# Logarithm of the input factor in the exponents; one run of rotation products, sums by halves, sines ahead of the gate

## What is computed

```
proj = xn @ in_proj_w.T          # z, x, B, C, dt, theta, lam
dt = softplus(dt_raw + dt_bias);  A = -exp(A_log);  lam = sigmoid(...)
tc = cumsum(theta, axis=1)
rope(v) = [v1*cos(tc) - v2*sin(tc), v1*sin(tc) + v2*cos(tc)]
Bm, Cm = rope(rms(B)+B_bias), rope(rms(C)+C_bias)       # per head
alpha = exp(dt*A);  gamma = lam*dt;  beta = (1-lam)*dt*alpha
h_t = alpha*h + gamma*(x_t B_t) + beta*(x_{t-1} B_{t-1});   y_t = h_t C_t
y = rms((y + x*D) * silu(z), norm_w) @ out_proj_w.T
out = u + y * silu(fp8_linear(xn) + ffn_bias)
```

## Time and profile before

| | |
|---|---|
| median of three executions | 1283.85 us |
| the profiled execution | 1283.93 us, span 1282.2 us |
| busy: TensorE / VectorE / ScalarE / GpSimd | 88% / 93% / 58% / 57% |
| TensorE weight loads busy | 64% |
| DMA engines | 46.4% |
| granted TensorE clock, mean | 0.967; 1.0 throughout the units |

### The profile page before, as it was taken

One profiled execution on the slowest core, in us unless ns is written; L12 is line 12 of the kernel. 1 busy time (PEld: TensorE's weight loads), 2 busy tenths in 40 slices (PEclk: granted clock), 3 DMA queues, 4 the chain that ended last, 5 costly groups with the idle time before them and its releaser, 6 DMA issues. The chain is left out here.

```text
span 1282.2 us, 30215 instructions
## 1 busy us (share of the span) xinstructions
PE 1124.5 (88%) x11410; PEld 819.9 (64%) x11410; DVE 1195.0 (93%) x1925; ACT 737.9 (58%) x1133; POOL 736.5 (57%) x588
## 2 busy tenths in 40 slices
PE   3876499998999999999999899989999899999996
PEld 3752366766666666666666666666667666666665
DVE  7998599998999899998999899999999899989994
ACT  4776155555655565556655655556555656556553
POOL 4000166666666666565766576657666576666664
PEclk9876699999999999999999999999999999999998
DMA  8534464345544355445544454346444455434441
GB/s 187 185 99 123 111 139 102 97 93 123 126 117 97 74 146 113 100 104 108 112 107 103 114 130 102 88 96 150 108 109 91 107 122 117 100 88 90 106 98 26
DMA packets 88468, 141.26 MB, mean 110 GB/s; under 512 B 16099, under 2 KB 35268, under 8 KB 88004
## 3 DMA queue, kind: packets, MB, share of 16 engines
q1 hardware_dynamic: 88323, 139.33, 46.4%
HBM read 57.89 MB, written 12.58 MB: 55 GB/s over the span
## 5 line engine op out<-in xcount | busy, mean ns | idle before, releaser
L1412 POOL TENSOR_TENSOR rot<-part 128x512 f32<-128x512 f32 x256 | 375.5, 1468 | 507.7 <-DVE part L1220 507.1
L1220 DVE SCALAR_TENSOR_TENSOR part<-bcs,k_prmT,k_trig 128x512 f32<-128x512 f32 x512 | 502.0, 1028 | 22.1 <-DMA bcs<-bc_t 12.4
L1353 ACT ACTIVATE E<-d 128x512 f32<-128x512 f32 x256 | 151.8, 593 | 192.5 <-PE d L1051 192.5
L1062 PE MATMUL s<-rot 64*128 64x128 f32 x2048 | 150.4, 286 | 26.6 <-POOL rot L1412 26.3
L1388 ACT ACTIVATE sz<-r 128x512 f32<-128x512 f32 x128 | 76.5, 597 | 165.5 <-PE r L1137 165.4
L1062 PEld LDWEIGHTS s<-rot 64*128 64x128 f32 x2048 | 127.6, 189 | 64.6 <-issue 64.4
L1238 DVE TENSOR_TENSOR M<-s,E 128x512 f32<-128x512 f32 x256 | 163.7, 679 | 2.4 <-PE s L1062 1.8
L1421 POOL TENSOR_TENSOR ce<-rot,eb 128x512 f32<-128x512 f32 x128 | 160.1, 1271 | 0.0
L1465 POOL TENSOR_TENSOR sqa<-sqa,sq 128x512 f32<-128x512 f32 x112 | 142.5, 1272 | 16.2 <-ACT sq L1358 7.8
L1036 PE MATMUL r<-k_w_zx,xns 128*128 128x256 f32 x512 | 131.8, 383 | 12.5 <-DMA xns<-xn_t 12.5
L1149 PE MATMUL y<-M,xk 128*64 128x128 f32 x2048 | 140.1, 279 | 0.0
(11 more groups left out here) (243 smaller groups left out, 1671.1 us busy)
## 6 DMA issues: line engine op xcount, KB each, us to landing
k_trig<-k_tri SPq DMA_DIRECT2D x512, 128.0 KB, 2.4
eb<-ecum_rows SPq DMA_DIRECT2D x128, 256.0 KB, 4.7
bcs<-bc_t SPq DMA_DIRECT2D x16, 256.0 KB, 3.9
bcs<-bc_t SPq DMA_DIRECT2D x32, 128.0 KB, 3.9
a_big<-in_L_attn_u SPq DMA_DIRECT2D x4, 512.0 KB, 6.3
xn_t<-a_xnT SPq DMA_DIRECT2D x1, 2048.0 KB, 10.7
tc_t<-a_tcT SPq DMA_DIRECT2D x1, 2048.0 KB, 15.9
bc_t<-a_tmp SPq DMA_DIRECT2D x1, 2048.0 KB, 8.5
```

Of the source, the lines that this page charges most:

```text
L1062: last = nc.tensor.matmul(Sp[j][:, k], rot[rows, q % 2, p, 0, k], rot[rows, q % 2, p, 1, k], start=True, stop=True)
L1220: nc.vector.scalar_tensor_tensor(out=part[:, 2 * p + f, :], in0=bcs[:, (t + q // NQ) % 2, 2 * w + f, :], scalar=col, in1=trig[:, p, 1 - f, ...
L1353: nc.scalar.activation(E[:, h % 2, :], Dp[:], ACT.Exp).then_inc(e_ready, 1)
L1412: nc.gpsimd.tensor_tensor(rot[:, q % 2, p, w, :], part[:, 2 * p, :], part[:, 2 * p + 1, :], ALU.add).then_inc(rot_ready, 1)
```

## The change

- The factor `kk` no longer multiplies x. Its logarithm, cut in three bf16 parts, is stored to scratch (`logs_d`), loaded per slice into twelve more rows of `pick` (`OWN_L`), and so enters the exponents, which have 123 rows in place of 111. The decay to the chunk's end, `dec`, is multiplied by `kk` in `prepare`.
- `xk` is now a plain copy of x, made by ScalarE (`x_copy`, two a unit). VectorE makes only `xc`, two passes in place of four, and waits for the copy (`x_copied`).
- VectorE's list of a unit: angle, state, M 2 and 3, `x_scaled` twice, all eight products in a run, then as before.
- GpSimd's sums wait for a half of the run: sums 0 and 1 for the first four products, 2 and 3 for all eight. `ce` goes in front of the sums.
- ScalarE: copies behind the decays, then the sines, then the two Silus.
- TensorE: x 0 and x 1 one behind the other, project as a whole after them. The last project of a slice and the sum of squares move into unit 0 of the next slice; the latter goes into bank y0.
- Norm: `norm_start` behind M 3, `norm_seeded` within the run, `norm_refined` behind the squares of unit 0, `normalised` in unit 1 in front of the copies.

```diff
-D_ROWS = OWN_S + 3 * CS
+OWN_L = OWN_S + 3 * CS
+D_ROWS = OWN_L + 3 * CS
...
# prepare, GpSimd
+            for i in range(2):
+                pool.wait_ge(log_cut, i + 1)
+                nc.gpsimd.tensor_tensor(s[2]..., s[2]..., cum3[:, :, H * i:H * i + H], ALU.subtract).then_inc(log_left, 1)
+            pool.wait_ge(dec_done, 1)
+            nc.gpsimd.tensor_tensor(K["dec"][:], K["dec"][:], kk[:], ALU.mult).then_inc(log_left, 1)
# prepare, ScalarE
             for g in (0, 2):
+                if g == 2:
+                    act.wait_ge(kk_done, 2)
+                    nc.scalar.activation(s[2], kk[:], ACT.Ln).then_inc(log_left, 1)
...
+            log_part(0)
             for t in range(NS):
                 if t + 2 < NS:
                     gate_input(t + 2)
+                if t in (1, 3):
+                    log_part((t + 1) // 2)
...
+                if t in (3, 4):
+                    act.wait_ge(cum_stored, 64)
+                    for g in (2 * t - 6, 2 * t - 5):
+                        act.wait_ge(logT_t, g + 1)
+                        nc.scalar.copy(cumT[:, 1024 * g:1024 * g + 1024], ...).then_inc(logT_out, 1)
# units, TensorE
-                    if q == 0:
-                        pe.wait_ge(ssq_taken, at(1, t, 0))
...
                     exponents(t, q, 3)
+                    if q == 0 and t > 0:
+                        square_sums(t - 1)
...
                         x_by_token(t, q + 1, 0)
-                    if q > 0:
-                        project(t, q - 1, (0, 1))
                     pe.wait_ge(hch, at(T8, t, 8 * q + 8))
                     if live(t, q + 1):
                         x_by_token(t, q + 1, 1)
-                    if q > 0:
-                        project(t, q - 1, (2, 3))
+                    if t + q > 0:
+                        project(t, q - 1, range(CS))
# units, VectorE
-                dve.wait_ge(x_ready, at(T2, t, 2 * q + i + 1))
+                dve.wait_ge(x_copied, at(T2, t, 2 * q + i + 1))
...
-                    if live(t, q + 1):
-                        rotation(t, q + 1, 0, 0, 0)
-                    if q == 0 and t > 0:
-                        norm_start(t - 1)
                     if live(t, q + 2):
                         angles(t, q + 2)
                     for c in range(CS):
                         state(t, q, c)
-                    if live(t, q + 1):
-                        rotation(t, q + 1, 0, 0, 1)
-                        x_scaled(t, q + 1, tn, 0)
-                        x_scaled(t, q + 1, tn, 1)
                     scores(t, q, 2)
                     scores(t, q, 3)
                     if q == 0 and t > 0:
-                        norm_seeded(t - 1)
+                        norm_start(t - 1)
                     if live(t, q + 1):
-                        for p, w in ((1, 0), (0, 1), (1, 1)):
+                        x_scaled(t, q + 1, tn, 0)
+                        x_scaled(t, q + 1, tn, 1)
+                        for p, w in ((0, 0), (1, 0), (0, 1), (1, 1)):
                             rotation(t, q + 1, p, w, 0)
                             rotation(t, q + 1, p, w, 1)
+                            if q == 0 and t > 0 and (p, w) == (1, 0):
+                                norm_seeded(t - 1)
# units, ScalarE
+            def x_copy(t, q, i):
+                act.wait_ge(x_ready, at(T2, t, 2 * q + i + 1))
+                act.wait_ge(y_ready, at(T2, t, 2 * q - 2))
+                nc.scalar.copy(xk[:, q % 2, 2 * i:2 * i + 2, :]..., R[i][:]).then_inc(x_copied, 1)
...
                     decays(t, q, 3)
+                    if q == 1 and t > 0:
+                        normalised(t - 1)
+                    if live(t, q + 1):
+                        x_copy(t, q + 1, 0)
+                        x_copy(t, q + 1, 1)
                     if q == 0 and t > 0:
                         root(t - 1)
+                    if live(t, q + 2):
+                        sines(t, q + 2)
                     for p in range(2):
...
-                    if live(t, q + 2):
-                        sines(t, q + 2)
...
-                    if q == 0 and t > 0:
-                        normalised(t - 1)
# units, GpSimd
-                pool.wait_ge(part_ready, at(T8, t, 8 * q + 2 * k + 2))
+                pool.wait_ge(part_ready, at(T8, t, 8 * q + 4 * w + 4))
...
+                    c_decayed(t, q)
                     if live(t, q + 1):
-                        sums(t, q + 1, 0)
-                    c_decayed(t, q)
-                    if q == 0 and t > 0:
-                        norm_refined(t - 1)
-                    if live(t, q + 1):
-                        for k in range(1, 4):
+                        for k in range(4):
                             sums(t, q + 1, k)
                     if q == 0:
                         ...
+                        if t > 0:
+                            norm_refined(t - 1)
```

More of the change, by code:

```diff
@@ L217, in _ @@
             fill(cum[MASK_ROWS:OWN_T], own[MASK_ROWS:OWN_T, :], 8)
-            fill(cum[OWN_S:D_ROWS], own[OWN_S:D_ROWS, :], 8)
+            fill(cum[OWN_S:OWN_L], own[OWN_S:OWN_L, :], 8)
+            fill(cum[OWN_L:D_ROWS], own_log[OWN_L:D_ROWS, :], 8)
             by_super = lambda a: a[:].rearrange("p (s t) -> p s t", s=NS)
@@ L242, in _ @@
                 sp.dma_start(gate_d[t], fgate[:, t % 2, :]).then_inc(gate_stored[t % 2], 16)
-            sp.wait_ge(masks_stored, 16 * 6)
+                if t == 5:
+                    sp.wait_ge(logT_out, 4)
+                    for i in range(3):
+                        sp.dma_start(logs_d.rearrange("t c i h s -> i h (t c) s")[i],
+                                     cumT[H * i:H * i + H, :].rearrange("h (x s) -> h x s", s=P)).then_inc(logs_stored, 16)
+            sp.wait_ge(masks_stored, 16 * 7)
             sp.wait_ge(dup_stored, 2 * DUP)
@@ L469, in _ @@
                 last.then_inc(g_t, 1)
+                if t in (3, 4):
+                    pe.wait_ge(log_cut, 3)
+                    for g in (2 * t - 6, 2 * t - 5):
+                        if t == 3:
+                            pe.wait_ge(cumT_a if g % 2 == 0 else cumT_v, 2)
+                        else:
+                            pe.wait_ge(logT_out, g - 1)
+                        for i in range(8):
+                            last = nc.tensor.transpose(ps_bf[g % 2][0:3 * H, i, :], cum3[:, 8 * g + i, :], K["ident_bf"][:])
+                        last.then_inc(logT_t, 1)
         @block.vector
@@ L820, in _, with units @@
                 nc.scalar.activation(fgate[:, t % 2, :], ps[2 + t % 2][:], ACT.Silu, scale=sc[:, 5:6]).then_inc(g_done, 1)
-def units(nc, K, u, scratch, cum_stored, out):
-    xn_d, tc_d, bc_d, cum_d, cumt_d, gate_d, ecum_d = scratch
+                if t in (3, 4):
+                    act.wait_ge(cum_stored, 64)
+                    for g in (2 * t - 6, 2 * t - 5):
+                        act.wait_ge(logT_t, g + 1)
+                        nc.scalar.copy(cumT[:, 1024 * g:1024 * g + 1024],
+                                       ps_bf[g % 2][0:3 * H].rearrange("p c t -> p (c t)")).then_inc(logT_out, 1)
+def units(nc, K, u, scratch, cum_stored, logs_stored, out):
+    xn_d, tc_d, bc_d, cum_d, cumt_d, gate_d, logs_d, ecum_d = scratch
     with ExitStack() as ctx:
@@ L1080, in project, with square_sums @@
                     last.then_inc(out_ready, 1)
+            def square_sums(t):
+                pe.wait_ge(yt_ready, at(T2, t, T2))
+                pe.wait_ge(sqa_ready, at(T2, t, T2))
+                for c in range(CS):
+                    last = nc.tensor.matmul(Yp[0][:, c:c + 1], sqa[:, c * P:c * P + P], K["ones"][:, 0:1],
+                                            start=True, stop=True)
+                last.then_inc(ssq_ready, 1)
             pe.wait_ge(xn_loaded, 16)
@@ L1174, in _ @@
                     exponents(t, q + 1, 1)
-                project(t, NQ - 1, range(CS))
-                pe.wait_ge(sqa_ready, at(T2, t, T2))
-                pe.wait_ge(e_ready, at(T4, t, T4 + 2 if live(t, NQ) else T4))
-                for c in range(CS):
-                    last = nc.tensor.matmul(Dp[:, c:c + 1], sqa[:, c * P:c * P + P], K["ones"][:, 0:1],
-                                            start=True, stop=True)
-                last.then_inc(ssq_ready, 1)
+            project(NS - 1, NQ - 1, range(CS))
+            square_sums(NS - 1)
         @block.vector
@@ L1331, in _ @@
             act.sem_inc(absd, 3)
-            for s in (e_ready, sz_ready, sq_ready, acc_done):
+            for s in (e_ready, x_copied, sz_ready, sq_ready, acc_done):
                 act.sem_inc(s, 1)
@@ L1485, in program @@
         cum_stored = ctx.enter_context(nc.semaphore("cum_stored"))
-        prepare(nc, K, dram, scratch, cum_stored)
-        units(nc, K, dram[0], scratch, cum_stored, out)
+        logs_stored = ctx.enter_context(nc.semaphore("logs_stored"))
+        prepare(nc, K, dram, scratch, cum_stored, logs_stored)
+        units(nc, K, dram[0], scratch, cum_stored, logs_stored, out)
```

68 lines of the change are left out of this document (45 added, 23 removed).

## The result

The changed kernel takes 1324.16 us (median of 4 runs, 1322.77 to 1324.35) where the kernel before takes 1282.77: ratio 1.0318, 95% interval 1.0298 to 1.0338. It is slower by 3.2%. The profiled execution of it has a span of 1322.6 us.

The account below looks back on a forecast made before the run. VectorE's list bounded the old kernel; after the change a four-engine loop of 17.29 us would. 1283.93 + 17.9 (units, slice extras) + 4 (prepare) - 1 (start of units) = 1304.8, 1305 us; likeliest 1288 to 1328, 8 in 10: 1236 to 1330.

Parts of the forecast that it names:

- The sign: Whole kernel: slower 0.64, within 0.3% 0.12, faster by over 0.3% 0.24.
- the once-a-slice term: Extra time in units 0, 1 and 1 to 2 of each slice: 4.6 us a slice, seven times.
- The loop of 17.29 us a unit: Eight products, sum 2, TensorE from s 0 to x 1, copy, x_scaled: 16.97 plus 0.32 of hand-overs; bounds 17.2 to 17.7.
- The wait of the last x_scaled for the copy: End of the loop: VectorE idle before the second x_scaled until ScalarE's 0.59 us copy of x 1 is done.
- One unit taken for all: Units: the loop worked out from one unit's timeline, 17.29 us, was applied to all 61 units.
- The term for `finished`: Unit 1 to 2: GpSimd's `finished` waits for `normalised`, delaying `ce` and sum 0: 3.0 us, bounds 0.6 and 3.2.
- prepare: Stage before the units: added ScalarE and GpSimd work costs 4 us, bounds 0 to 10; start of units gives -1.
- The third table load: ScalarE, sines before Silus: one more load of 1.28 us per unit, 64 in all, hidden with some 3 us of cover.
- the rival with switches of twice the price: ScalarE: each of three table switches costs twice 1283 ns, about 0.5 us a unit, +30: 1335 us; chance 8%.
- The fifth product isn't held: VectorE's run: it gets in ahead of sum 1, or the loop is otherwise shorter, 16.2 us: 1240 us; chance 14%.
- VectorE's list decides: Units: engine loop shorter than VectorE's 15.75 us, so the dropped passes are all gain: about 1210 us; chance 8%.

Follow-up runs that it names:

- The run with eight places: Changed kernel with eight places in `part` for the partial products and all four GpSimd sums behind the whole run of products: 1313.74 us, ratio 1.0251.
- the last three runs: Logarithm and copy in the old order, x 1 before project: 1288.95 us; also products 1 and 2 behind the state: 1293.33; changed kernel, product run cut in two: 1408.21.
- order alone: Kernel before with only the new order (one run of eight, sums held, both x in a row), without logarithm or copy: 1426.19 us, ratio 1.1117.

## Why the prediction came out as it did

The sign, the range and the mechanism of the loop held; the number, 1305 against 1324, is made of errors in both directions. That it is no further off is partly luck: with the once-a-slice term at its measured size the forecast would have been 1287.

- **The loop of 17.29 us a unit: right.** Measured 17.26 to 17.27 in the odd slices. Its parts are there: the fifth product's wait (1.39, foreseen 1.31), one held product, the wait of TensorE in front of s 0, VectorE's idle time in front of M 0, M 1 and the angle. The run with eight places shows that the loop goes through the sums, the run with free sums that this costs 38 us with all that follows. The wait of the last x_scaled for the copy is there too, but small: the copy of x 1 ends at 694.38 and the pass begins at 694.41, 0.11 us after the first one is done. So the chain through VectorE's M 0 to M 3 and the one through x 1 and the copy arrive nearly together, which the prediction had left open. In all VectorE is idle 1.08 us outside the run, not 1.5; its busy share is 81%, not 87.

```profile
693.79 0.59 ACT L1406 COPY xk<-r 128x512 f32<-128x512 f32 x1 [0.28 <-PE r L1087]
694.41 0.69 DVE L1256 TENSOR_TENSOR xc<-r,k_cc 128x512 f32<-128x512 f32 x1
```

- **One unit taken for all: +5.6.** The earlier trace rows are a unit of an odd slice. In the even ones TensorE has 32 products of the state's term and not 24, and the unit takes 17.50, as it already took 17.27 and not 17.01 before. 61 units at the mean of 17.38 instead of 17.29. The mean of 17.52 in the earlier trace rows was put down to the first units of a slice alone.
- **Once a slice 4.6 us: mis-sized.** Without the clock, 1074.6 us are left for the 61 units, 14.4 over 61 x 17.38: 2.1 a slice; the kernel before has some 2.8 over its own plain units. -18. The term for `finished` was set at 3.0, as if GpSimd waited for `normalised`; it is 0.9, by 1.1 us of `ce` beside the run.
- **The clock: a missing term, +25.8.** The prediction foresaw TensorE waiting 1 to 1.5 us in one piece and gave it no price, since the unit of the earlier trace rows, with waits of 0.38 and 0.86 us, doesn't show what a longer one does. This is the step that failed, and the largest one: a wait of 1.76 to 1.99 us was taken for time in which nothing else happens, and the run with the wait filled shows that it cost 23 us in clock.
- **prepare: +6.1.** 9.1 instead of 4 - 1. The collisions with GpSimd's passes were named but counted as spread over idle time; by the run without them, 4.7 of the 9.1 are theirs. The load and the logarithm on ScalarE, 1.28 + 1.06, were counted so too, but stand in front of the sines, whose table load comes at 101.25 in place of 99.00.
- **The third table load: right**, hidden as foreseen. 1283 ns, 62 more of them (the prediction had 64). The timeline shows load and sine end to end, so the rival with switches of twice the price falls:

```profile
694.93 1.28 ACT L1393 ACT_TABLE_LOAD   x1
696.22 0.63 ACT L1393 ACTIVATE k_tri<-ang 128x512 f32<-128x512 f32 x1
```

The Trainium skill's page ScalarE activation tables: per-element evaluation and per-set limits, section Table sets in the compiler and the runtime, has the loads placed for the longest run of functions, which would be two a unit here; the trace has three. Of the drain that ScalarE: Activation LUTs, section What ACT_TABLE_LOAD costs, adds to a load, these rows show nothing: the sine starts 0.01 us after the load's end.

- **The rivals.** "The fifth product isn't held" was priced at 1240. With eight places it isn't held, and the run measured 1314, because the sums of C end no earlier; with the sums free it was 1286, because then three products are held and VectorE's list is the loop again at 17. "VectorE's list decides" (1210) would have needed a GpSimd that is not in the way; the last three runs show how far that is.

The sum of the steps: 1304.8 + 5.6 - 18 + 25.8 + 6.1 = 1324.3.

## What to carry to other kernels

Before an engine is relieved, look for the loops that are nearly as long as its list: here three of them seem to lie within a microsecond (VectorE's list, TensorE's way to x 1 and, argued only, GpSimd's `ce` behind sum 0), and 1.2 us taken off the first brought nothing. Price an order by the wait that it leaves in one piece on TensorE, not only by the sum of the waits: with 1.76 to 1.99 us in front of s 0 the clock cost 22 us more than before and the longer schedule 9.4, and with two waits of 0.45 and 0.77 it fell in 4 of 62 units only. And read the repeating pattern over two slices before one unit stands for all.

## What the runs showed of the hardware

That TensorE's clock falls to its lower level behind a wait was not expected. In the kernel before, where most waits are 0.38 to 0.86 us, it fell in 3 of 62 units, and two of the three have one of its longest waits, 1.43 and 1.46. In the changed kernel it fell in 17: in none of the 7 with a wait of 1.5 us in front of s 0, in 11 of the 49 with 1.75 to 1.99, in all 6 with 2.04 to 2.96. It fell in 35 where most waits are 2.15 to 2.4 (run cut in two), in 38 with 2.4 to 3.0 (order alone), and with the wait filled down to 0.37 in none. With eight places there are three waits near each other, mostly of 0.44 to 0.65, 0.57 and 0.44 us, and it fell in 12. The stretch at the lower level takes in one or two groups of products and makes 1.6 us a time in the changed kernel. What decides in which of two like units it falls stays open: 217.17 and 234.68 above have the same wait, and only behind the second does it fall.

Nor had it been expected that a one-input pass of VectorE is held up like the two-input ones (the expectation of the run without GpSimd's passes calls all three two-input): L657, a TENSOR_SCALAR of 0.43 us, took 2.46 beside GpSimd's third pass in `prepare`.

```profile
114.38 2.46 DVE L657 TENSOR_SCALAR a_half<-a_big 128x512 fp8e4<-128x512 f32 x1
...
113.76 2.80 POOL L334 TENSOR_TENSOR k_dec<-k_dec,a_kk 128x1024 f32<-128x1024 f32 x1
```
